# First experts' second biases added in VectorE's copy out of PSUM, with the end of that stage reordered and the values' bias on GpSimd

## The reference

```python
# second stage: 8 experts, the best two of each token
topk_w, topk_idx = jax.lax.top_k(probs, 2)
topk_w = topk_w / topk_w.sum(axis=-1, keepdims=True)
combine = (one_hot(topk_idx, 8) * topk_w[..., None]).sum(axis=1)
out = 0.5 * gelu(flat @ shared_W + shared_b)
for e in range(8):
    h = gelu(flat @ W1[e] + b1[e])
    out = out + combine[:, e:e + 1] * (h @ W2[e] + b2[e])
out = layernorm(out) * gamma + beta
x = layernorm(x + out)
# third stage
v = jnp.einsum('bsd,hdk->bhsk', x, Wv) + bv
```

## Time and profile before

| | |
|---|---|
| median of 3 runs | 1654.23 us (1653.32, 1654.23, 1657.09) |
| profiled execution, its own time | 1653.79 us |
| its span in the trace | 1652.0 us |
| mean granted TensorE clock | 0.898 of full speed |
| TensorE busy | 1332.8 us (81%) |
| VectorE busy | 1195.5 us (72%) |
| ScalarE busy | 920.5 us (56%) |
| GpSimd busy | 932.1 us (56%) |

### The profile page before, as it was taken

How to read it: one execution, slowest core, us unless ns; L and a number is a source line. 1 busy time by engine, 2 the same in 40 slices (tenths; PEclk the granted TensorE clock), 3 DMA queues, 4 the chain that set the end, 5 groups by cost and what they waited for, 6 DMA issues and landing times. The chain is left out here.

```text
span 1652.0 us, 25211 instructions
## 1 busy us (share of the span) xinstructions
PE 1332.8 (81%) x7251; PEld 717.1 (43%) x7251; DVE 1195.5 (72%) x2207; ACT 920.5 (56%) x1736; POOL 932.1 (56%) x771
## 2 busy tenths in 40 slices
PE   5848888888788989998917999999999998812756
PEld 2313333333333359998914244444343343212643
DVE  6999999999999553233465988888888886160325
ACT  5746666666665644456566067675566666601423
POOL 2479998998999017370744021214563654874773
PEclk9879989998999978999958599999999999955867
DMA  2019100000000025786719211211221114301317
GB/s 69 0 63 345 49 0 0 0 0 0 0 0 0 1 64 153 199 242 186 206 41 262 64 32 31 61 31 31 74 64 35 44 40 106 59 10 46 105 51 255
DMA packets 123041, 124.87 MB, mean 76 GB/s; under 512 B 31182, under 2 KB 97979, under 8 KB 120304
## 3 DMA queue, kind: packets, MB, share of 16 engines
q1 hardware_dynamic: 101032, 99.70, 21.8%
q0 software_dynamic: 10240, 15.79, 3.3%
q10 hardware_dynamic: 11656, 8.00, 1.6%
HBM read 78.52 MB, written 50.91 MB: 78 GB/s over the span
## 5 line engine op out<-in xcount | busy, mean ns | idle before, releaser
L2103 DVE TENSOR_REDUCE t_negm<-t_ps 128x1 f32<-128x512 f32 (+4 forms) x624 | 370.1, 642 | 56.6 <-PE t_ps L2371 35.2
L2080 ACT ACTIVATE t_PT<-t_ps_s 128x1024 f32<-128x1024 f32 (+3 forms) x384 | 292.1, 811 | 202.5 <-PE t_ps_s L2390 201.6
L493 POOL TENSOR_TENSOR s_HC<-s_H,X 128x1024 f32<-128x1024 f32 x128 | 307.0, 2416 | 39.2 <-DVE s_H L614 31.2
L658 PE MATMUL ps_y<-s_HC,ident 128*128 128x512 f32 x512 | 262.4, 637 | 21.1 <-POOL s_HC L493 19.4
L2008 POOL TENSOR_SCALAR_AFFINE_SELECT t_PT<-t_PT 128x512 f32<-128x512 f32 x128 | 82.8, 648 | 275.9 <-ACT t_PT L2080 275.3
L2371 PE MATMUL t_ps<-heads 96*128 96x512 bf16 (+3 forms) x640 | 201.1, 341 | 9.3 <-DVE t_negm L2103 7.6
L2390 PE MATMUL t_ps_s<-heads 96*128 96x512 bf16 (+3 forms) x768 | 180.9, 328 | 4.0 <-ACT t_PT L2080 2.2
L2405 PE MATMUL t_ps_c<-t_PT,t_VG 128*32 128x512 f32 (+3 forms) x1536 | 163.7, 499 | 1.7 <-ACT t_CT L2036 1.1
L554 ACT ACTIVATE s_dA<-m_DT,s_A 128x512 f32 (+1 forms) x192 | 127.5, 712 | 60.4 <-DVE s_H L614 59.5
L658 PEld LDWEIGHTS ps_y<-s_HC,ident 128*128 128x128 f32 x512 | 94.4, 197 | 122.9 <-issue 66.8
L1992 POOL DMA_INDIRECT slots<-X,t_idx_s x128 | 127.2, 994 | 34.9 <-issue 34.3
(11 more groups left out here) (348 smaller groups left out, 2393.9 us busy)
## 6 DMA issues: line engine op xcount, KB each, us to landing
f_w<-in_W_dram SPq DMA_DIRECT2D x93, 256.0 KB, 5.5
heads<-token_expert_rows SPq DMA_DIRECT2D x8, 1024.0 KB, 9.8
token_expert_rows<-X SPq DMA_DIRECT2D x42, 192.0 KB, 2.7
heads<-q_parts SPq DMA_DIRECT2D x42, 192.0 KB
heads<-k_parts SPq DMA_DIRECT2D x14, 576.0 KB
expert_rows<-X SPq DMA_DIRECT2D x27, 192.0 KB, 2.4
f_XS<-expert_rows SPq DMA_DIRECT2D x19, 256.0 KB, 3.5
expert_rows_out<-f_YB ACTq DMA_DIRECT2D x19, 256.0 KB
```

The costliest lines, as they stand in the source:

```text
L493: nc.gpsimd.tensor_tensor(HC[:, g % RING], H[:, g % RING], row_wide(C_sb[:, g % RING, :], 2), ALU.mult).then_inc(s_hc, 2)
L658: nc.tensor.matmul(ps_y[c][:], ident[:], HC[:, g % RING, c, :], start=g == 0, stop=g == N - 1, skip_group_check=True).then_inc(s_y, 1)
L2080: nc.scalar.activation(PT[:, n % RP, 2 * p:2 * p + 2, 0:wd], src, ACT.Exp, scale=DK ** -0.5).then_inc(s_exp, 1)
L2103: nc.vector.tensor_reduce(out, ps_1[use % BANKS1][:, 0:h * width].rearrange("p (h k) -> p h k", h=h), AX.X, ALU.max, negate=True).then_inc ...
```

## The change

1. The sum of second biases is taken away: `comb`, its transpositions and copies, the eight matmuls of `b2_sum`, the clearing of `b2big`. `biases` becomes `halved`, which only halves the accumulator. SyncE loads `b2` once, repeated over all partitions (512 KB), without waiting for GpSimd.
2. The copy out of a quad becomes, for each block, a register load of the block's expert and an addition of 128 x 128 that reads `ps_y` and the row of `b2_rows` which that register names, and writes `YB`. VectorE waits for `b2` before the first, and for `eid`.
3. Behind the loop the order of VectorE's and ScalarE's work is another one. The last unit (tiles 28 to 31) gets both its scalings and its residual on VectorE, by the functions that group 0 uses; its normalisations wait until the 28 tiles before it are done.
4. In the projections the values are multiplied without a bias, and GpSimd adds it to each chunk of `Vt` after ScalarE's copy (eight additions of 128 x 512).

The diff, cut to what changes the work:

```diff
                 sp.dma_start(w2[:, e, :].rearrange("p (m n) -> p m n", n=P), io["W2"][e].rearrange("(m p) n -> p m n", p=P)).then_inc(s_w2, 16)
-            sp.wait_ge(s_z, 1)
-            for t in range(NT // 2):
-                sp.dma_start(b2big[t * E0:(t + 1) * E0, t, :], io["b2"]).then_inc(s_b2, 16)
+            sp.dma_start(b2_rows[:].rearrange("p e n -> p (e n)"),
+                         io["b2"].rearrange("(a e) n -> a (e n)", a=1).broadcast_to([P, E0 * P])).then_inc(s_b2, 16)
...
             nc.gpsimd.iota(blk_i[:], pattern=[[1, max(GBLK)]], base=0, channel_multiplier=0).then_inc(s_k, 1)
-            nc.gpsimd.memset(b2big[:], 0.0).then_inc(s_z, 1)
             pool.wait_ge(s_xz, filled(keep, s_xz))
...
             scaled(1, 1, range(*TAIL[1]))
-            for i in range(2, 5):
-                scaled(0, 2, range(i * PER, (i + 1) * PER))
-                if i > 2:
-                    x2_copy(i - 1)
+            scaled(0, 2, range(2 * PER, 3 * PER))
             tail_root(2, 1)
+            scaled(2, 1, range(*TAIL[2]))
+            x2_copy(2)
+            tail_root(1, 2)
+            scaled(0, 2, range(3 * PER, 4 * PER))
+            tail_root(2, 2)
+            scaled(0, 2, range(4 * PER, 5 * PER))
+            x2_copy(3)
+            scaled(1, 2, range(*TAIL[1]))
             x2_copy(4)
-            tail_root(1, 2)
-            scaled(2, 1, range(*TAIL[2]))
-            scaled(1, 2, range(*TAIL[1]))
-            tail_root(2, 2)
+            tail_root(3, 1)
+            scaled(2, 2, range(*TAIL[2]))
             x2_copy(5)
-            scaled(2, 2, range(*TAIL[2]))
-            tail_root(3, 1)
-            scaled(3, 1, range(*TAIL[3]))
             x2_copy(6)
             tail_root(3, 2)
-            scaled(3, 2, range(*TAIL[3]))
             x2_copy(7)
...
                 link(nc.vector.tensor_tensor(wt[:, 2, :], wt[:, 2, :], wt[:, 1, :], ALU.mult))
-                for r in range(2):
-                    also(nc.vector.tensor_tensor(oh[:, r], oh[:, r], wide(wt[:, 1 + r, :], E0), ALU.mult))
-                dve.wait_ge(s_rt, n)
-                nc.vector.tensor_tensor(comb[:], oh[:, 0], oh[:, 1], ALU.add).then_inc(s_cb, 1)
-
-            def turned_shares():
-                for h in range(2):
-                    dve.wait_ge(s_ct, 2)
-                    nc.vector.tensor_copy(combT[:, h, :], ps_r[:, h * P:(h + 1) * P]).then_inc(s_ctc, 1)
-
-            def biases(i):
-
-                dve.wait_ge(s_b2m, i + 1)
+
+            def halved(i):
+
                 part = ACC[:, i * PER:(i + 1) * PER, :].rearrange("p t n -> p (t n)")
-                nc.vector.scalar_tensor_tensor(out=part, in0=part, scalar=0.5, in1=ps_r[:], op0=ALU.mult, op1=ALU.add).then_inc(s_a0, 1)
+                nc.vector.tensor_scalar(part, part, 0.5, None, ALU.mult).then_inc(s_a0, 1)
...
                     dve.wait_ge(s_ys[q % RY], 16 * turns(q - RY, RY))
-                cols = QUADS[q][2] * P
-                nc.vector.tensor_copy(YB[:, q % RY].rearrange("p a n -> p (a n)")[:, 0:cols], ps_y[q % 2][:, 0:cols]).then_inc(s_yc, 1)
+                if q == 0:
+                    dve.wait_ge(s_b2, 16)
+                    dve.wait_ge(s_ei, 1)
+                elif q == GQ[1][0]:
+                    dve.wait_ge(s_ei, 2)
+                for a in range(QUADS[q][2]):
+                    k = FIRSTB[q] + a
+                    e = dve.value_load(eid[0:1, k:k + 1], min_val=0, max_val=E0 - 1)
+                    b2_e = b2_rows[:, bass.ds(e, 1), :].rearrange("p a n -> p (a n)")
+                    last = nc.vector.tensor_tensor(YB[:, q % RY, a, :], ps_y[q % 2][:, a * P:(a + 1) * P], b2_e, ALU.add)
+                last.then_inc(s_yc, 1)
...
-            def residual():
-                tiles = range(*GROUPS[0])
-                inverse(1, *GROUPS[0])
+            def residual(span):
+                tiles = range(*span)
                 at = [mark(nc.vector.scalar_tensor_tensor(out=ACC[:, t, :], in0=ACC[:, t, :], scalar=mv[:, t, 0:1], in1=gamma[:],
...
                     at.append(mark(nc.vector.bn_stats(stats[:, t, :], ACC[:, t, :])))
-                variance(*GROUPS[0], aggregate(tiles, at))
+                return aggregate(tiles, at)
...
-            def normalise():
-                inverse(2, *GROUPS[0])
-                for t in range(*GROUPS[0]):
+            def normalise(span):
+                for t in range(*span):
                     nc.vector.tensor_scalar(ACC[:, t, :], ACC[:, t, :], mv[:, t, 0:1], rstd[:, t:t + 1],
...
                     shares()
-                elif q == 1:
-                    turned_shares()
-                elif q < 2 + NCH // 2:
-                    biases(2 * q - 4)
-                    biases(2 * q - 3)
+                elif 2 <= q < 2 + NCH // 2:
+                    halved(2 * q - 4)
+                    halved(2 * q - 3)
                 if q == BESIDE:
...
                 elif q == BESIDE + 2:
-                    residual()
+                    inverse(1, *GROUPS[0])
+                    variance(*GROUPS[0], residual(GROUPS[0]))
                 elif q == BESIDE + 3:
-                    normalise()
+                    inverse(2, *GROUPS[0])
+                    normalise(GROUPS[0])
                 elif NQ - 4 <= q < NQ - 1:
...
             variance(*TAIL[2], combine(6))
-            done = tail_residual(5)
             scale_and_shift(2, 1)
-            variance(*TAIL[1], done)
+            variance(*TAIL[1], tail_residual(5))
+            variance(*TAIL[2], tail_residual(6))
             scale_and_shift(1, 2)
-            variance(*TAIL[2], tail_residual(6))
             scale_and_shift(2, 2)
             variance(*TAIL[3], combine(7))
-            scale_and_shift(3, 1)
-            variance(*TAIL[3], tail_residual(7))
-            scale_and_shift(3, 2)
+            inverse(root_of(3, 1), *TAIL[3])
+            variance(*TAIL[3], residual(TAIL[3]))
+            inverse(root_of(3, 2), *TAIL[3])
+            dve.wait_ge(s_fin, TAIL[3][0])
+            normalise(TAIL[3])
...
-            def comb_turned():
-                pe.wait_ge(s_cb, 1)
-                for h in range(2):
-                    nc.tensor.transpose(ps_r[:, h * P:(h + 1) * P], comb[:, h * 16:(h + 1) * 16, :].rearrange("p t e -> p (t e)"), ident[:]).then_inc(s_ct, 1)
-
-            def b2_sum(i):
-                pe.wait_ge(s_b2, 16 * NT // 2)
-                pe.wait_ge(s_ctc, 2)
-                if i:
-                    pe.wait_ge(s_a0, i)
-                cols = b2big[:, (i % 4) * PER:(i % 4 + 1) * PER, :].rearrange("p t n -> p (t n)")
-                nc.tensor.matmul(ps_r[:], combT[:, i // 4, :], cols, start=True, stop=True).then_inc(s_b2m, 1)
-
...
                 down(k)
-                q, nth = QOF[k], k - FIRSTB[QOF[k]]
-                if q == 1 and nth == 0:
-                    comb_turned()
-                elif 2 <= q < 2 + NCH // 2 and nth < 2:
-                    b2_sum(2 * q - 4 + nth)
             pe.wait_ge(s_xc, NQ)
...
                 pool.sem_clear(used)
+            pool.wait_ge(s_w, 16 * 6)
+            for i in range(NCH):
+                rows = Vt[:, i * PER:(i + 1) * PER, :]
+                pool.wait_ge(s_vt, i + 1)
+                nc.gpsimd.tensor_tensor(rows, rows, row_wide(v_b, PER), ALU.add).then_inc(s_vb, 1)
...
                     pe.wait_ge(s_vt, i - 1)
-                nc.tensor.matmul(ps_v[k][:].rearrange("p (t n) -> p t n", n=P), keep["ones"][:], row_wide(v_b, PER),
-                                 start=True, stop=False, skip_group_check=True)
                 for t in range(PER):
                     mm = nc.tensor.matmul(ps_v[k][:, t * P:(t + 1) * P], X2[:, i * CH + t * P:i * CH + (t + 1) * P], w[2],
-                                          start=False, stop=True, skip_group_check=True)
+                                          start=True, stop=True)
                 mm.then_inc(s_v, 1)
```

More of the change, by code:

```diff
@@ L913, in ffn @@
         sh_b = sb("sh_b", [P, P])
-        b2big = sb("b2big", [P, NT // 2, P])
+        b2_rows = sb("b2_rows", [P, E0, P])
         gamma = sb("gamma", [P, P])
@@ L923, in ffn @@
         wt = sb("wt", [P, 3, NT])
-        comb = sb("comb", [P, NT, E0])
-        combT = sb("combT", [P, 2, P])
         trif = sb("trif", [P, P])
@@ L967, in ffn @@
         s_w2 = sem("w2_loaded")
-        s_w, s_b2, s_z, s_k, s_lg, s_sh, s_tr = (sem(n) for n in (
-            "weights", "b2_loaded", "b2_zeroed", "constants", "logits", "shared", "x_turned"))
+        s_w, s_b2, s_k, s_lg, s_sh, s_tr = (sem(n) for n in (
+            "weights", "b2_loaded", "constants", "logits", "shared", "x_turned"))
         s_l, s_gelu, s_x1t, s_rt, s_d, s_exp, s_m, s_rk = (sem(n) for n in (
             "logits_copied", "shared_gelu", "x_token_major", "route", "difference", "gate_exp", "mask", "ranks"))
-        s_ix, s_ei, s_cb, s_ct, s_ctc, s_b2m, s_a0 = (sem(n) for n in (
-            "slots", "block_experts", "comb", "comb_t", "comb_t_copied", "b2_sum", "acc_begun"))
```

(3 more changed lines are left out.)

## The result

The change makes the kernel slower: 1666.26 us median of 7 runs (1657.68 to 1670.35) against 1654.23 of 7 runs of the kernel before; the ratio is 1.0062, 95% interval 1.0041 to 1.0083, so 10.3 us, between 7 and 14. The forecast was slower, 1661. The profiled execution has a span of 1664.9 us, 12.9 above the span of before.

The account below looks back on a forecast made before the run. It took TensorE to be the bound in the expert loop, with the copy in delayed by longer copies out. Terms 5.4 + 2.2 + 4.8 - 4.4 - 0.8 = +7.2 us on 1653.8 gave 1661.0, range 1648 to 1678.

Parts of the forecast that it names:

- What bounds it: Expert loop: TensorE looks like the bound; longer copies out delay the copy in, so TensorE waits 0.9 us per full quad.
- c: VectorE's queue cost of one block's addition (register load, checks, address, issue): taken as 0.8 us, bounds 0.3 and 1.25.
- hidden loads: Rival, VectorE's copy out: c stays under about 0.45 and the copy in arrives in time; about 1648 us, chance 0.20.
- loads that wait for the additions: Rival, VectorE's copy out: each load waits 0.35 us for the addition in front, c 1.1 to 1.25; 1680 to 1689, chance 0.08.
- Quads 1, 2 to 5, 6 to 10: Expert loop: +0.7, -2.9 and +1.3 us, from matmuls and transpositions removed against new TensorE waits of 0.9 per full quad.
- Quads 11 to 13: Expert loop, VectorE already the bound: each copy out holds its queue 2.85 us longer, passed on twice through ScalarE's variance waits; +5.7.
- Quads 14 and 15: Expert loop: 8.91 us becomes 8.6 and 5.79 becomes 6.7; +0.6.
- Gathers: Second group's gathers: quad 15's copy out ends later, +2.2 us; the last two copies out delay the last 16 gathers, +4.8.
- The stage's end: Behind the loop: reordered, bound by the last gather's landing, the stage's last copy ends at 862.9 instead of 867.28; gain 4.4 us.
- Projections: Projections: without bias matmuls ScalarE bounds four chunks, some 0.3 us each; GpSimd's additions lie beside other work; -0.8 taken.
- The rival with GpSimd holding VectorE: Projections: GpSimd's additions stop VectorE's differences, chunks 4.0 us instead of 3.2 for some four chunks; 1664 us, chance 0.04.

Follow-up runs that it names:

- no loads: Changed kernel with expert 0's second bias added to every block, so no register loads or register addresses on VectorE: 1648.66 us, ratio 0.9960.
- copy in first: Changed kernel with the copy in of quad q + 2 issued ahead of the copy out of quad q, loads unchanged: 1654.64 us, ratio 0.9991.
- both mendings: Changed kernel with the copy in ahead of the copy out and each turn's register loads ahead of VectorE's wait for the outputs: 1651.45 us, ratio 0.9969.
- loads spread: Changed kernel, copy in ahead of copy out, loads ahead of the wait, those for turns 10 to 13 and 18 to 20 four turns earlier: 1648.38 us, ratio 0.9964.
- old values' bias: Changed kernel with the values' bias put back on TensorE as a matmul, GpSimd's additions taken out: 1663.76 us, ratio 1.0050.
- old end: Changed kernel with the order of before behind the loop: 1669.57 us, ratio 1.0092.
- new end alone: Kernel before with only the new order of VectorE's and ScalarE's work behind the loop: 1651.87 us, ratio 0.9982.

## Why the prediction was right

- **What bounds it.** Right: TensorE waits for the copy in 17 times, 13.4 us in all, behind a copy out that is longer than the 3.26 it leaves. Without the loads the whole loss goes. One reading beside it was off: of the 0.54 in which each of quads 6 to 10 was said to wait, the row cited has only (40.71 - 39.06) / 5 = 0.33 of idle time.
- **c**, the term on which all hung, was taken as 0.8, between 0.3 and 1.25; it is 0.75. SyncE's row of the same chain was the right one to go by, and the load itself, 0.302, was near SyncE's 0.271. A nearer row for the load was overlooked: TensorE's own queue loads the same number in the kernel before, in 0.303. The floor of some 600 ns for a register load (the Trainium skill, DMA: Bandwidth & Descriptors, Latency and other measured facts) is not borne out by any of these rows. The rivals with hidden loads and with loads that wait for the additions fall with it: each load takes its place in the queue, and it starts 0.03 after the start of the addition in front of it, not after its end.
- **Quads 1, 2 to 5, 6 to 10:** +0.7, -2.9, +1.3 forecast; +0.8, -2.0, +0.9 in the stretches. The reason given for the second was half of it: the matmuls' time goes not only to waits for copies in. In the four kernels in which these waits are gone or nearly so (no loads, copy in first, both mendings, loads spread) quads 0 to 5 take 47.97 to 49.44 in place of 49.90, so 0.5 to 1.9 less. A supply that the prediction left out of its sum stands behind them: GpSimd's scatters of the second group, for which SyncE waits with quad 5's weights behind it.
- **Quads 11 to 13:** +5.7 forecast, +4.8 measured (26.88 to 31.71). That the numbers agree is luck. The waits named are there, but the two of ScalarE grew by 1.5 and 1.0, not by 2.85 each, and TensorE's idle time by 1.8. The other 3.0 are busy time at a lower clock, which the forecast did not have: 0.53 for 6.5 us behind TensorE's wait of 3.42, an estimated 6.5 x 0.47 = 3.1. Nor does this part come with the change each time: behind the same wait of 3.42 the clock was 0.77 for 6.5 us with the old values' bias, and a kernel with the loop of before has 0.75 there (the last section).
- **Quads 14 and 15:** +0.6 forecast, +3.3 measured (14.70 to 17.97): the worst of the loop's terms. In quad 15 TensorE waits 2.17 for the copy in, where 0.9 was forecast, and the clock is 0.83, an estimated 9.88 x 0.17 = 1.7. With the old values' bias, the same loop, the clock there is 1.00.
- **Gathers:** +2.2 and +4.8 forecast; +1.4 (5.70 to 7.06 from the end of quad 15) and +3.4. The first 32 gathers take 42.3 in both (828.92 - 0.83 - 785.83; 844.66 - 4.26 - 798.08), and the last 16 wait for the store of the last two copies out, as forecast.
- **The stage's end:** -4.4 forecast, -5.4 measured, -5.1 and -5.3 in the table for the kernels that differ in this alone (33.30 against 38.36, 32.85 against 38.19).
- **Projections:** -0.8 forecast, +1.0 in the two traces, -0.6 in the means over all twelve, nothing that can be told in the time. The rival with GpSimd holding VectorE named the right line and the right mechanism, but had it in four chunks; it came in one. The Trainium skill (SBUF — State Buffer, Who interferes with whom) has it that an instruction of VectorE with two inputs in SBUF and one of GpSimd that reads SBUF exclude each other. The 3.59 in place of 1.47 agrees with that.

The sum of the terms was +7.2, their sum in the trace is +8.2, and the measured difference 10.3 (7 to 14). So the forecast was right in what it rests on, c and the waits for the copy in, and closer in the sum than in its parts. Quads 11 to 13 were forecast with waits that are mostly not there; without the clock, an estimated 3.1 + 1.7 in this one trace, the terms would add up to some 3.4.

## What to carry to other kernels

A register load on VectorE cost its whole chain in the queue, here 0.46 us beyond the work, and it cost where it stood: ahead of the wait it went mostly into idle time, behind the wait 85 loads cost about 1% (a ratio of 1.0062, against 0.9960 without them). An engine that waits a lot is not therefore free: look at how long it has between what releases it and what others wait for, here 3.26 us. And work taken from the engine that looks like the bound is worth little where a supply (here scattered rows and the weights queued behind them) arrives only just in time: 6.9 us of matmuls went, and of the time no more than 3.1 us, by the 95% interval.

## What the runs showed of the hardware

- VectorE's register load took 0.302 us, and with checks, address and issue an addition followed the last one after 0.75; without loads between them, additions of 128 x 128 followed each other after some 0.2 (four in 0.88).
- Two differences of VectorE, each with both inputs in SBUF, took 3.59 us beside GpSimd's additions in place of 1.47.
- Behind a wait of TensorE of 3.42 us the granted clock was 0.53 over 6.5 us in the changed kernel, 0.55 with the old end and 0.77 with the old values' bias, all with the same loop; these lie between the two levels, so the clock was at the lower one (1.2 of 2.4 GHz) for part of the time. Behind the wait of 2.42 in the same place of the kernel before it was 1.00, and behind one of 2.43 in "new end alone", with the same loop, it was 0.75:

```profile
753.90:760.40 6.50, 6.48 (x44) 6.49 (x45) 0.67 (x3) 4.18 (x16) 0.00 (x0) 0.75 0.34 92
```

So the same code gets different clocks in different executions, and the length of this one wait does not settle which.
